# Sorting rows for experts: the weight tables are taken out of the sort and put behind slot 0's up product

## The reference, cut to what matters

```python
logits = jnp.einsum('th,eh->te', x, gate_w)
probs = jax.nn.softmax(logits, axis=-1)
...
# TOP_K = 2: per row the two best experts and their weights, which sum to 1;
# y += weight * (silu(x @ w1_gate.T) * (x @ w1_up.T)) @ w2.T for both
```

## Time and profile before

| what | value |
|---|---|
| median of 3 runs | 1621.25 us (1614.23 to 1623.17) |
| the profiled execution, its own time | 1608.78 us |
| its span from the first to the last instruction | 1607.1 us |
| PE busy | 1493.9 us, 93% |
| DVE busy | 923.4 us, 57% |
| ACT busy | 721.0 us, 45% |
| POOL busy | 606.0 us, 38% |
| mean granted TensorE clock | 0.972 of full |

### The profile page before, as it was taken

How to read it: one execution, slowest core, us unless ns; L and a number is a source line. 1 busy time by engine, 2 the same in 40 slices (tenths; PEclk the granted TensorE clock), 3 DMA queues, 4 the chain that set the end, 5 groups by cost and what they waited for, 6 DMA issues and landing times. The chain is left out here.

```text
span 1607.1 us, 34125 instructions
## 1 busy us (share of the span) xinstructions
PE 1493.9 (93%) x11983; PEld 1262.4 (79%) x12004; DVE 923.4 (57%) x2133; ACT 721.0 (45%) x1784; POOL 606.0 (38%) x473
## 2 busy tenths in 40 slices
PE   6999999999699999997799999999999779999996
PEld 5787887887478898895588787887887558999996
DVE  4677677776732234223687978878878762222221
ACT  3766666666222234333555644564546302333332
POOL 5655465465323334431222332233223403333342
PEclk9999999999799999998899999999999969999999
DMA  6364454463569877543001011010100138787753
GB/s 218 105 206 163 175 204 149 177 210 138 206 210 329 242 221 225 125 67 106 14 21 34 21 34 54 21 34 21 43 32 21 35 130 270 218 266 204 190 97 49
DMA packets 95917, 212.36 MB, mean 132 GB/s; under 512 B 7216, under 2 KB 7216, under 8 KB 94512
## 3 DMA queue, kind: packets, MB, share of 16 engines
q1 hardware_dynamic: 76736, 166.58, 29.7%
q0 software_dynamic: 17472, 40.90, 12.8%
q10 hardware_dynamic: 1584, 3.15, 0.5%
HBM read 136.94 MB, written 73.66 MB: 131 GB/s over the span
## 5 line engine op out<-in xcount | busy, mean ns | idle before, releaser
L1299 PE MATMUL bank<-ring,halves 128*128 x1872 | 332.0, 326 | 3.5 <-ACT halves L1139 3.5
L1299 PEld LDWEIGHTS bank<-ring,halves 128*128 128x128 f32 x1872 | 302.6, 188 | 10.6 <-issue 4.5
L499 POOL TENSOR_TENSOR arena<-arena 128x1024 f32<-128x1024 f32 x64 | 123.8, 1934 | 142.2 <-DVE arena L579 140.6
L1697 DVE SCALAR_TENSOR_TENSOR arena<-arena 128x256 f32<-128x256 f32 x240 | 128.4, 577 | 19.3 <-ACT arena L1916 16.5
L1593 POOL TENSOR_TENSOR arena<-arena 128x1024 f32<-128x1024 f32 x16 | 31.3, 1957 | 280.1 <-ACT arena L1970 240.8
L792 PE MATMUL bank<-arena 128*128 128x128 f32 x1024 | 125.0, 281 | 1.8 <-ACT arena L692 0.8
L711 ACT ACTIVATE arena<-arena 128x256 f32<-128x256 f32 x256 | 126.3, 499 | 0.0
L792 PEld LDWEIGHTS bank<-arena 128*128 128x128 f32 x1024 | 119.0, 195 | 7.7 <-issue 3.6
L1119 POOL DMA_INDIRECT out_dram<-arena x39 | 61.7, 1582 | 154.2 <-issue 90.8
L1119 POOL DMA_INDIRECT mid_rows<-arena x39 | 61.8, 1585 | 148.2 <-issue 94.3
L1139 ACT ACTIVATE halves<-bank 128x512 fp32r<-128x512 f32 x78 | 46.6, 597 | 157.2 <-PE bank L1282 157.2
(11 more groups left out here) (285 smaller groups left out, 3265.8 us busy)
## 6 DMA issues: line engine op xcount, KB each, us to landing
ring<-expert_halves SPq DMA_DIRECT2D x16, 4352.0 KB, 18.8
expert_halves<-expert_high SPq DMA_DIRECT2D x16, 1088.0 KB, 8.7
expert_halves<-expert_rest SPq DMA_DIRECT2D x16, 1088.0 KB, 10.8
arena<-in_w_dram SPq DMA_DIRECT2D x8, 1088.0 KB, 6.6
normalised_rows<-arena SPq DMA_DIRECT2D x33, 256.0 KB, 2.0
arena<-in_x_dram SPq DMA_DIRECT2D x32, 256.0 KB, 2.7
arena<-mid_rows SPq DMA_DIRECT2D x32, 256.0 KB, 2.8
w_in_raw<-in_in_w_dram SPq DMA_DIRECT2D x16, 290.0 KB, 6.6
```

The source lines that it names most:

```text
L499: nc.gpsimd.tensor_tensor(held, held, spread(rinv[:, HG * g:HG * g + HG], 2, 2 * P), ALU.mult)\
L1299: last = nc.tensor.matmul(bank[1 + 2 * par + part][:, 0:INTER], rows_parts[a][:, par, k * P:k * P + P], weights(at, b, (2 * k + part) * IN ...
L1697: last = nc.vector.scalar_tensor_tensor(out=slot[:, j], in0=cin[:, c, k:k + PAIR], scalar=taps[:, c, k:k + 1], in1=slot[:, j], op0=ALU.mul ...
```

## The change

In both sorts `by_slot`'s row-number part is made first and alone: per part one table of one-hots and one product, and `lists` multiplies 40 columns instead of 120. DVE works out `sort.turn` (two small steps) before it waits for the list instead of behind it. `index`, `place`, `needed` and `ends` are made; then bank 5 is cleared; then the weights are split into high and rest; then, in four parts, each weight table is made by one scalar_tensor_tensor out of the row-number table ("above 0.5" times the weight). Between the second and the third part DVE does `rest_of_rows(0, 0)`. PE multiplies the weight tables, 80 columns wide, into bank 6 with a second call of `lists` (32 more matmuls), placed behind turn(1) and ahead of up(1). DVE waits for that (`w_lists_made`), adds the columns into `weight`, and then goes on with `rest_of_rows(1, 1)` and `product(0, 0)`. In moe_a SP waits for `w_lists_made` before it issues the 16 loads of the Mamba block's weights.

```diff
-    rank_bank, list_bank = bank[3], bank[7]
+    rank_bank, list_bank, w_bank = bank[3], bank[7], bank[6]
...
                 if e == RING and in_w is not None:
+                    sp.wait_ge(w_lists_made, 1)
...
-                link(nc.vector.tensor_copy(sort.w_parts, sort.w[:, 0:K]))
-                link(nc.vector.tensor_tensor(sort.w[:, K:2 * K], sort.w[:, 0:K], sort.w_parts, ALU.subtract))
                 for j in range(0, K * T, PART):
...
                     nc.vector.tensor_tensor(sort.by_slot[:, part, 0], one_hot, spread(core.rowid[:, of_tile], 2, SLOTS + 1),
-                                            ALU.mult)
-                    nc.vector.tensor_tensor(sort.by_slot[:, part, 1], one_hot,
-                                            spread(sort.w_parts[:, j // T, of_tile], 2, SLOTS + 1), ALU.mult)
-                    nc.vector.tensor_tensor(sort.by_slot[:, part, 2], one_hot,
-                                            spread(sort.w[:, K + j // T, of_tile], 2, SLOTS + 1), ALU.mult)\
-                        .then_inc(tables_ready, 1)
+                                            ALU.mult).then_inc(tables_ready, 1)
...
+                link(nc.vector.tensor_scalar(sort.turn, sort.owner, float(RING), -float(RING), ALU.is_ge, ALU.mult))
+                link(nc.vector.tensor_tensor(sort.turn, sort.turn, sort.owner, ALU.add))
                 dve.wait_ge(lists_made, 1)
...
-                link(nc.vector.tensor_copy(weight, list_bank[:, SLOTS + 1:2 * SLOTS + 1]))
-                link(nc.vector.tensor_tensor(weight, weight, list_bank[:, 2 * SLOTS + 2:3 * SLOTS + 2], ALU.add))
+                nc.vector.memset(bank[5][:], 0.0).then_inc(cleared, 1)
+                link(nc.vector.tensor_copy(sort.w_parts, sort.w[:, 0:K]))
+                link(nc.vector.tensor_tensor(sort.w[:, K:2 * K], sort.w[:, 0:K], sort.w_parts, ALU.subtract))
+                dve.wait_ge(tables_ready, 4)
+                for j in range(0, K * T, PART):
+                    if j == 2 * PART:
+                        rest_of_rows(0, 0)
+                    part, of_tile = slice(j, j + PART), slice(j % T, j % T + PART)
+                    here = sort.by_slot[:, part, 0].bitcast(F32)
+                    nc.vector.scalar_tensor_tensor(out=sort.by_slot[:, part, 1], in0=here, scalar=0.5,
+                                                   in1=spread(sort.w_parts[:, j // T, of_tile].bitcast(F32), 2, SLOTS + 1),
+                                                   op0=ALU.is_gt, op1=ALU.mult)
+                    nc.vector.scalar_tensor_tensor(out=sort.by_slot[:, part, 2], in0=here, scalar=0.5,
+                                                   in1=spread(sort.w[:, K + j // T, of_tile], 2, SLOTS + 1),
+                                                   op0=ALU.is_gt, op1=ALU.mult).then_inc(w_tables_ready, 1)
+                dve.wait_ge(w_lists_made, 1)
+                link(nc.vector.tensor_copy(weight, w_bank[:, 0:SLOTS]))
+                link(nc.vector.tensor_tensor(weight, weight, w_bank[:, SLOTS + 1:2 * SLOTS + 1], ALU.add))
 
             sort_rows()
-            nc.vector.memset(bank[5][:], 0.0).then_inc(cleared, 1)
-            for par in range(2):
-                rest_of_rows(par, par)
+            rest_of_rows(1, 1)
             product(0, 0)
...
-            lists()
+            lists(list_bank[:, 0:SLOTS + 1], slice(0, 1), tables_ready, lists_made)
...
             turn(1)
+            lists(w_bank[:, 0:2 * (SLOTS + 1)], slice(1, 3), w_tables_ready, w_lists_made)
             pe.wait_ge(cleared, 1)
```

More of the change, by code:

```diff
@@ L1071, in run_slots @@
     chain = sem("sort_chain")
+    w_tables_ready, w_lists_made = sem("w_tables"), sem("w_lists")
     both_ready, ranks_made, gap_ready, exp_ready = sem("both"), sem("ranks"), sem("gap"), sem("exp")
@@ L1252, in sort_rows @@
                                                op0=ALU.add, op1=ALU.add).then_inc(index_ready, 1)
-                link(nc.vector.tensor_scalar(sort.turn, sort.owner, float(RING), -float(RING), ALU.is_ge, ALU.mult))
-                link(nc.vector.tensor_tensor(sort.turn, sort.turn, sort.owner, ALU.add))
                 link(nc.vector.tensor_scalar(sort.again, sort.turn, float(RING), -float(RING), ALU.is_ge, ALU.mult))
@@ L1348, in rank_last, with lists @@
                     .then_inc(ranks_made, 1)
-            def lists():
+            def lists(out, columns, tables, done):
                 n = TOPK * TILES
@@ L1353, in lists @@
                     if j % PART == 0:
-                        pe.wait_ge(tables_ready, j // PART + 1)
-                    last = nc.tensor.matmul(list_bank[:, 0:3 * (SLOTS + 1)], sort.at_spot[:, j // TILES, j % TILES],
-                                            sort.by_slot[:, j].rearrange("p c s -> p (c s)"),
+                        pe.wait_ge(tables, j // PART + 1)
+                    last = nc.tensor.matmul(out, sort.at_spot[:, j // TILES, j % TILES],
+                                            sort.by_slot[:, j, columns].rearrange("p c s -> p (c s)"),
                                             start=(j == 0), stop=(j == n - 1))
-                last.then_inc(lists_made, 1)
+                last.then_inc(done, 1)
             stay_busy(core, bank[6], 3)
```

## The result

Over 22 runs each the changed kernel takes 1606.82 us (1604.24 to 1614.58) and the kernel before 1615.89 us (1609.07 to 1623.62). The ratio is 0.9947, 95% interval 0.9932 to 0.9962: 9 us faster. The two profiled executions differ by less: a span of 1602.8 us against 1607.1.

A forecast was written before the change was run, and what follows sets the result against it. The prediction took moe_b's chain of adds, started by slot 0's result and slowed by weight loading, as the bound. Per stage -4.2 + 3.15 - 1.0 = -2.05, twice -4.1, from 1621.25 to 1617.1 us, range 1605 to 1625.

The forecast's parts named there:

- What bounds the kernel: End of each expert stage: slot 0's result time and the weight loading beside the chained adds set the time.
- The adds never catch up: In moe_b: its end is the start of add 0 plus a chain of 38 intervals.
- The part that gets shorter: Each sort, up to turn(0): the row-number list is read earlier, so turn(0) comes 4.2 us earlier.
- The part that is added: Between turn(1) and up(1): 32 weight-list matmuls of 80 columns at 0.121 us; loss 3.15 us per stage.
- The stall for the rest of the rows: In up(1), at its ninth matmul: the rest of the weights is late by some 0.15 us.
- rival 3: Narrow matmuls at 81 ns, full clock in lists and second filler: -4.45 us per stage, 1612.4 us in all; chance 0.18.
- The transfers: Weight loads beside the chain of adds: 3.15 us more loading done beforehand, 0.32 per us, chain 1.0 us shorter per stage.
- The sum: Per stage -4.2 + 3.15 - 1.0 = -2.05, twice -4.1 us, from 1621.25 to 1617.1 us; chance 0.45.
- Rival 1: Chain of adds: the relief doesn't come, -1.05 us per stage, 1619.2 us in all; chance 0.22.
- Rival 2: Between turn(1) and slot 0's result, both sorts: clock falls, up to +7.2 us, 1628.5 us without relief; chance 0.15.
- Rival 4: At turn(0): filler or gather holds it, gain 3.3, -1.2 us per stage, inside the forecast's range; no chance of its own.

The follow-up runs named there:

- e3: Changed kernel, but expert 1's load waits for the weight list instead of turn(1); ratio to the kernel before 0.9995, 1613.3 us.
- e6: Kernel before, with expert 1's load issued at turn(0) instead of turn(1), sort untouched; ratio to the kernel before 0.9969, 5 us faster.
- e1: Kernel before with the change in moe_a's sort alone; ratio to the kernel before 0.9975, 1611.1 us.
- e2: Kernel before with the change in moe_b's sort alone; ratio to the kernel before 0.9973, 1612.2 us.
- e5: Changed kernel with only 8 of the 32 weight-list matmuls, so the result is incomplete; ratio to the kernel before 0.9929, 1602.7 us.
- e8: Changed kernel with the first 16 weight-list matmuls ahead of turn(0), behind 10 fillers instead of 18; ratio to the kernel before 0.9988, 1612.7 us.
- e9: Changed kernel with 16 weight-list matmuls directly ahead of turn(0), behind 12 fillers and TensorE's register loads; ratio to the kernel before 0.9963, 1608.2 us.
- e10: Changed kernel, 16 weight-list matmuls ahead of turn(0) behind 12 fillers and register loads, expert 1's load at turn(0); ratio to before 0.9938, 1603.0 us.

## Why the prediction was right, and where it was too small

**What bounds the kernel: right in the main, incomplete.** e3 and e6 move in effect one load and change the time by 8 and 5 us; the time of slot 0's result and the loading beside the adds are what counts. What was missing is TensorE's pace. "The adds never catch up" holds for moe_b of the kernel before, but by 2.5 us only, and nothing in the forecast said so. In moe_a they catch up in every profile, also in that of the kernel before: there the seven adds ahead of the last one are released by ACT, most of them 6.7 us apart. What the adds cost in moe_a is what they hold back ACT, and through it TensorE, before that: 261.4 us from the first to the last result against 252.0 in moe_b, of which other work of that stage may have a share.

**The part that gets shorter, forecast 4.2 a stage: mis-sized.** The reader of the list came 4.5 us earlier in moe_b, as worked out to 0.3. But turn(0) came 5.2 us earlier there. The forecast had 4.8 for it by the gather and took 4.2, since the filler might hold it; with the list running without gaps the clock stayed full, 18 fillers took 4.06 us and not 5.70, and the gather was the last to come. In moe_a the clock did fall and the filler held turn(0); it came 4.3 us earlier, inside the 3.3 to 4.6. (The late end of the filler in moe_b, 1325.5 in the forecast, is 1325.2 by the terms given.)

**The part that is added, forecast 3.15: mis-sized.** up(1) started 3.93 us behind turn(1) instead of 1.47, that is 2.46, and `turn_act` lost 2.33 (6.10 for 3.77). Two causes: 32 matmuls of 80 columns took 3.6 us, 0.112 to 0.114 each and not 0.121, and they began 0.33 after turn(1)'s start, where the sum let them begin at the end of its record, 0.60. The stall for the rest of the rows came as forecast (0.18 for 0.15). By the pace that the Trainium skill gives for 128 columns ("TensorE: Matmul & The Clock Gate", the section on the back-to-back issue gap), 81 ns, an estimate is 2.6 us; the trace says 3.6, so that part of rival 3 fell. Its other part, a clock that stays full through the lists and the second filler, came true in moe_b and not in moe_a.

**The transfers, forecast 1.0 a stage: mechanism right, both factors off.** The load's lead over the first add grows by just what is added between turn(1) and the first add, so by 2.3 us (9.6 to 11.9) and not 3.15. In moe_b 1.6 came out, 0.7 per us and not 0.32. The estimate counted load 1 alone; it left out that load 1 also finished 2 us sooner, so load 2 moved by 4.35 us (8.1 to 3.75). By the forecast's own 0.32 those make 1.4, an estimate. The 1.6 is a difference of two means of three profiles that scatter by 1.5 us, so its size is rough; that there is a relief rests on e3 and e6.

**The sum.** In moe_b the three parts are -5.2 + 2.3 - 1.6 = -4.5 instead of -2.05; moe_a about the same by the times (e1: 4.0, e2: 4.4). Rival 1, no relief, fell with e3. Rival 2, a clock that falls between turn(1) and slot 0's result, didn't happen in the change (32 matmuls in 3.75 us in both sorts); a falling clock ahead of that place did happen in e5, e8, e9 and e10. Rival 3's sum, -4.45 a stage, is what was measured, with 4.8, 1.85 and 1.5 for the 5.2, 2.3 and 1.6, though its reason for the middle one was wrong. Rival 4 held in moe_a, where a filler held turn(0), and cost 0.2 us (in e5's moe_a the gather gave 17.43 us against 17.65); in moe_b none did.

That the time fell into the range owes something to luck. The measured 1606.8 us is 10.3 below the forecast of 1617.1: 5 of them because the change gave 9 us and not 4.1, and 5.4 because the median of three that the forecast started from, 1621.25, is 1615.9 over 22 runs. The profiled execution, 1608.8, lay 7 us on the other side. And the prediction gave only 0.20 to what came, faster by over 0.5%.

## What to carry to other kernels

When a stage ends in a chain of transfers that wait for one another, look at what else is on the DMA engines when the chain begins: here 5.5 us more lead for one weight load was worth about half of the whole change (e6), and it is in the main a change of one number in a wait. Work out also how long the chain would be if nothing held it, by the pace of the engine that feeds it: it can't give more than what lies above that. When work is taken out of a latency path and put beside the steady work, price it by the slot's own wait that it covers, and see what instruction that nobody waits for (register loads here) was hidden in the place that it leaves. And where one sum over two profiles doesn't fit the times, compare stage by stage over several profiles: stages with unchanged code differed here by up to 9 us.

## What had not been expected

Matmuls with a new weight load of 128 columns each ran at 0.121 us with 8, 40 and 120 moving columns, but at 0.114 with 80 (32 in 3.65, or 3.59 from the first to up(1)'s first weight load, 0.112). Why is open.

The stages that nobody touched scatter by as much as the 4.5 us that the change gives a stage, and more: attention 431.6 to 437.4 us (437.4 in e5), Mamba 569.3 to 572.4, moe_a's chain 263.3 to 272.6 with the code of before. The cause stays open, also that of the 272.6.
